# One block for the first two stages of a decoder layer, with hand-laid buffers and an early start of the second stage, and a start and an end of the experts by token tile

## What is computed

```python
x = x + attention(layernorm(x), w_qkv, w_out, alibi_slopes)        # stage 1, causal, 16 heads of 32
  probs = num / (sum(num) + 1e-6), num = 0.5 * (1 + s * rsqrt(1 + s * s))
q = layernorm(x) @ W_q;  k, v = context @ W_k, context @ W_v       # stage 2, 8 heads of 64
x = x + softmax(where(mask, q @ k.T / 8, -FLT_MAX)) @ v @ W_o + b_o
s = softmax(layernorm(x) @ w_router)                               # stage 3: top 2 of 8 experts,
x = x + sum_e weight_e * (gelu(xb_e @ w1_e) @ w2_e) + bias         # each takes 896 tokens
```

## Time and profile before

| | us |
|---|---|
| median of 3 runs | 3380.05 (3374.13 to 3383.58) |
| the profiled execution | 3391.78 |
| its span (first to last instruction) | 3390.1 |
| PE busy | 3071.0 (91%) |
| DVE busy | 1669.1 (49%) |
| ACT busy | 1351.4 (40%) |
| POOL busy | 732.2 (22%) |
| mean granted clock of PE | 0.951 of full speed |

### The profile page before, as it was taken

One profiled execution on the slowest core, in us unless ns is written; L12 is line 12 of the kernel. 1 busy time (PEld: TensorE's weight loads), 2 busy tenths in 40 slices (PEclk: granted clock), 3 DMA queues, 4 the chain that ended last, 5 costly groups with the idle time before them and its releaser, 6 DMA issues. The chain is left out here.

```text
span 3390.1 us, 52927 instructions
## 1 busy us (share of the span) xinstructions
PE 3071.0 (91%) x19340; PEld 2500.3 (74%) x19340; DVE 1669.1 (49%) x3816; ACT 1351.4 (40%) x2297; POOL 732.2 (22%) x564
## 2 busy tenths in 40 slices
PE   5889999865999999999999839999999999999997
PEld 4667777754777777777777628887888788878886
DVE  5888888843555565555555623232223232323232
ACT  5677777743555555555555411111111111111111
POOL 0000000001112222121221123333333333333333
PEclk9889999977999999999999859999999999999999
DMA  2011111114111111111110022222222222222222
GB/s 95 23 34 44 43 43 43 44 50 145 37 37 43 36 51 52 36 37 42 48 54 23 17 70 72 61 83 70 74 61 83 70 74 63 81 72 72 66 78 59
DMA packets 96191, 193.80 MB, mean 57 GB/s; under 512 B 18656, under 2 KB 28640, under 8 KB 94016
## 3 DMA queue, kind: packets, MB, share of 16 engines
q1 hardware_dynamic: 80912, 160.78, 15.6%
q0 software_dynamic: 15152, 31.26, 4.4%
HBM read 144.19 MB, written 47.82 MB: 57 GB/s over the span
## 5 line engine op out<-in xcount | busy, mean ns | idle before, releaser
L1619 DVE CAST f_hh<-f_hf 128x448 fp32r<-128x448 f32 x256 | 116.8, 456 | 893.2 <-ACT f_hf L1643 860.5
L1643 ACT ACTIVATE f_hf<-f_h 128x448 f32<-128x448 f32 x256 | 139.6, 545 | 1016.0 <-PE f_h L1679 983.2
L1566 POOL TENSOR_TENSOR f_w1l<-f_raw,f_w1h 128x512 fp32r<-128x512 f32 x130 | 183.4, 1411 | 829.2 <-DVE f_w1h L1601 829.1
L1695 PE MATMUL f_y<-f_w2h,f_hh 128*128 128x512 f32 x896 | 357.9, 399 | 0.0
L1695 PE MATMUL f_y<-f_w2h,f_hl 128*128 128x512 f32 x896 | 354.0, 395 | 0.0
L1695 PE MATMUL f_y<-f_w2l,f_hh 128*128 128x512 f32 x896 | 352.3, 393 | 0.0
L1266 ACT ACTIVATE c_s_sb<-c_s_sb,c_nmx 112x750 f32<-112x750 f32 x256 | 236.0, 922 | 188.9 <-DVE c_nmx L1095 186.5
L1679 PE MATMUL f_h<-f_xTh,f_w1h 128*128 128x448 f32 x1024 | 261.8, 378 | 32.3 <-ACT f_hf L1643 16.8
L1258 ACT COPY c_pT<-c_psum 125x672 f32<-125x672 f32 x256 | 184.7, 722 | 241.1 <-PE c_psum L1359 237.4
L1359 PEld LDWEIGHTS c_psum<-c_ident,c_s_sb 112*125 112x125 f32 x1536 | 198.2, 194 | 90.2 <-issue 84.5
L1679 PE MATMUL f_h<-f_xTl,f_w1h 128*128 128x448 f32 x1024 | 256.1, 373 | 0.0
(11 more groups left out here) (243 smaller groups left out, 5725.5 us busy)
## 6 DMA issues: line engine op xcount, KB each, us to landing
f_raw<-in_w SPq DMA_DIRECT2D x132, 512.0 KB
c_craw<-in_ctxT SPq DMA_DIRECT2D x16, 1125.0 KB, 5.1
a_x_in<-in_x SPq DMA_DIRECT2D x9, 896.0 KB, 5.7
a_xr<-in_x SPq DMA_DIRECT2D x8, 896.0 KB, 6.0
x_dram<-a_xr SPq DMA_DIRECT2D x8, 896.0 KB, 4.8
q_dram<-a_q SPq DMA_DIRECT2D x32, 224.0 KB, 5.3
c_q<-q_dram SPq DMA_DIRECT2D x16, 448.0 KB, 5.5
c_x<-x_dram SPq DMA_DIRECT2D x16, 448.0 KB, 4.6
```

What stands on the lines that cost most here:

```text
L1566: pool.tensor_tensor(w1s[1][:, n % NSLOT].rearrange("p k c -> p (k c)"), raw1[:, g % 2, n % 2, :], w1s[0][:, n % NSLOT].rearrange("p k c - ...
L1619: dve.tensor_copy(hs[0][:, l % 2, c * HC:c * HC + HC], hf[:, c, :]).then_inc(h_hi, 1)
L1643: act.activation(hf[:, c, :], H[:, 0:HC], ACT.Gelu_apprx_tanh).then_inc(free, 1)
L1695: mm = pe.matmul(Y[t][:], hs[a][:, l % 2, 128 * t:128 * t + 128], w2s[b][:, l % NSLOT, :], start=j == 0 and q == 0, stop=j == FB - 1 and q ...
```

## The change

*Buffers.* A class `Region` gives out SBUF addresses by hand, and a class `Handover` divides the memory into ten regions in which both stages lay their tensors, one over the other. It owns what is shared: the key and value weights, the context, `kT`, a separate buffer `stage` with four slots for weight pieces, the queries, the ten pieces' loads and splits, and one PSUM tensor (the units' banks are 4 and 5 for both stages, the transposes of the second stage 6 and 7). The semaphores with counts that a region is dead (`QKV_DEAD`, `outputs_dead`, `all_dead` and others) stand in place of the barrier.

*One block.* `self_attention` and `cross_attention` add their programs to one block, so each engine goes on from one to the other by itself.

*Last iteration of the first stage.* SP loads pieces 0 to 3 and the context behind `xr`. ACT rounds pieces 0 to 2 behind step 2, the context behind step 3, pieces 3 to 5 behind step 4; POOL makes the rests (DVE made both). PE does key units CK00, CK01, CK10 in step 6, CK11, CK20 in step 7 and CK21, CK30, CK31 between the last transposes. ACT takes them out. `normalise` comes before Y2 and Y3.

*Second stage.* `START` has the three value units alone, with the first scores ahead of them. Pieces 6 to 9 (output weights) are split by ACT and POOL in the first batch. The small loads and the mask are issued behind the first stage's last stores.

*Experts.* The first seven gathers have a semaphore each, and their transposes go to the seven banks `Y`. The scatters wait tile by tile for `ys_made`, each wait followed by a semaphore increment; the weight split ahead of them waits for the weight alone.

The diff, cut to its core (changes of indentation left out):

```diff
+    def load_piece(self, sp, n):
+        src, dst, k = self.pieces[n]
+        if n >= 4:
+            sp.wait_ge(self.w_lo, n - 3)
+        sp.dma_start(self.stage[:, n % 4, :], src[:, k, :]).then_inc(self.w_loaded[n % 4], 16)
+    def hi_of_piece(self, act, n):
+        src, dst, k = self.pieces[n]
+        act.wait_ge(self.w_loaded[n % 4], 16 * (n // 4 + 1))
+        act.copy(dst[0][:, k, :], self.stage[:, n % 4, :]).then_inc(self.w_hi, 1)
+    def lo_of_piece(self, pool, n):
+        pool.wait_ge(self.w_hi, n + 1)
+        pool.tensor_tensor(dst[1][:, k, :], self.stage[:, n % 4, :], dst[0][:, k, :].bitcast(F32), ALU.subtract).then_inc(self.w_lo, 1)
...
 def self_attention
-                     6: (["T2e2"], []),
-                     7: (["T2e3"], [])}
+                 6: (["T2e2"], ["CK00", "CK01", "CK10"]),
+                 7: (["T2e3"], ["CK11", "CK20"])}
-        END = ["OUT2", "OUT3", "Y0", "Y1", "Y2", "Y3", "T2c0", "T2c1", "T2c2", "T2c3", "Z0", "Z1", "Z2", "Z3"]
+    END = ["OUT2", "OUT3", "Y0", "Y1", "Y2", "Y3", "T2c0", "CK21", "T2c1", "CK30", "T2c2", "CK31", "T2c3", "Z0", "Z1", "Z2", "Z3"]
+    QKV_DEAD = (gen_full, product_number(NIT - 1, "last", "V3") + 1)
...
                     sp.dma_start(xr[:], one(x_v, i)).then_inc(xr_loaded, 16)
+            if kind == "last":
+                sp.wait_ge(x_loaded, (NIT + 1) * 16)
+                sp.wait_ge(mv_made[0], (NIT + 1) * TPI)
+                for n in range(4):
+                    handover.load_piece(sp, n)
+                sp.wait_ge(*QKV_DEAD)
+                handover.load_context(sp, 0)
...
+        for n in range(4, len(handover.pieces)):
+            handover.load_piece(sp, n)
             sp.wait_ge(stats_made[1], NIT)
             store_x1(NIT - 1)
+        sp.wait_ge(*handover.values_dead)
+        for e in range(2):
+            sp.wait_ge(q2_stored[e], 48)
+        handover.load_queries(sp, 0)
...
+                if kind == "last" and s in (2, 4):
+                    for n in range(3):
+                        handover.hi_of_piece(act, n + 3 * (s // 4))
+                if kind == "last" and s == 3:
+                    handover.hi_of_context(act, 0)
...
-            for unit in END[:6]:
+        for unit in END[:4]:
                 evacuate(NIT + 1, "end", unit)
             normalise(1, NIT - 1, xr, xn2)
...
 def cross_attention
-        START = [K(0, 0), K(0, 1), K(1, 0), K(1, 1), K(2, 0), V(0, 0), V(0, 1), V(0, 2), K(2, 1), K(3, 0)]
+    START = [V(0, 0), V(0, 1), V(0, 2)]
...
+        sp.wait_ge(*handover.outputs_dead)
             for dst, src in ((wr[:], w_r), (bo[:], b_o.partition_broadcast(R)), (bi[:], bias.partition_broadcast(R))):
                 sp.dma_start(dst, src).then_inc(small_loaded, 16)
-            sp.wait_ge(w_lo, 10)
...
             load_mask(0)
+        sp.wait_ge(*handover.all_dead)
             sp.dma_start(x1[:], x1_v[0]).then_inc(x_loaded, 16)
...
-            for unit in START:
-                evacuate(0, "start", unit)
             exponential(0, 0)
+        evacuate(0, "start", START[0])
             exponential(0, 1)
+        for unit in START[1:]:
+            evacuate(0, "start", unit)
+        for n in range(6, len(handover.pieces)):
+            handover.hi_of_piece(act, n)
...
 def experts
+                    pool.wait_ge(ys_made, it * (2 * NT) + p * NT + t + 1)
+                    pool.sem_inc(ys_seen, 1)
...
-                    if j == FB - 1:
-                        w = ((ys_made, it * (2 * NT) + NT * (p + 1)), (scattered, (it * 2 + p) * (16 * NT)))
...
-            pe.wait_ge(gathered, 16 * NT)
             for t in range(NT):
-                if t:
-                    pe.wait_ge(free, t)
-                rows(t)
+                pe.wait_ge(first_gathered[t], 16)
+                rows(t, Y[t])
```

More of the change, by code:

```diff
@@ L740, in cross_attention @@
-def cross_attention(nc, ctxT, mask, q2_dram, x1_dram, w_k, w_v, w_o, b_o, w_r, bias, out, xn_dram, table_dram):
+    sem = lambda n: ctx.enter_context(nc.semaphore("a_" + n))
+    at = lambda name: handover.region("a_", name)
+    sb = at("weights")
+    wqkv = [sb(f"wqkv{k}", [128, KC, 3 * C], F32R) for k in "hl"]
+    xT = [sb(f"xT{k}", [128, KC, TOK], F32R) for k in "hl"]
+    s_row = sb("s_row", [128, R])
+    x_in = at("rows")("x_in", [R, TPI, C])
+    ew = at("work")("ew", [128, 5 * EW])
@@ new lines, in self_attention, with units @@
+    START = ["T1c0", "T1c1", "T1c2", "T1c3", "Q0", "K0", "Q1", "K1", "V0", "V1", "Q2", "K2"]
+    END = ["OUT2", "OUT3", "Y0", "Y1", "Y2", "Y3", "T2c0", "CK21", "T2c1", "CK30", "T2c2", "CK31", "T2c3", "Z0", "Z1", "Z2", "Z3"]
+    def units(kind, s, half):
+        return [u for u in (PLAN_LAST if kind == "last" else PLAN)[s][half] if u not in NOT_YET.get(kind, ())]
+    BODIES = ("first", "second", "mid", "last")
+    ORDER = {k: [u for s in range(NG) for half in range(2) for u in units(k, s, half)] for k in BODIES}
@@ new lines, in step, with has_step, iterations @@
+    def step(i, s):
+        return (i, s) if s < NG else (i + 1, s - NG)
+    def has_step(kind, s):
+        return s < NG or kind != "last"
+    def iterations(eng, body):
+        body(0, "first")
+        body(1, "second")
+        with eng.Fori(2, NIT - 1) as i:
+            body(i, "mid")
+        body(NIT - 1, "last")
+    pieces = [(w_outT[:, k, :], wout, k) for k in range(KC)] + [(w_qT[:, k, :], wq2, k) for k in range(KC)]
+    stage = lambda n: ew[:, n * 3 * C:(n + 1) * 3 * C]
+    CONSTS = 6
@@ L741, in cross_attention @@
+def cross_attention(nc, ctx, block, handover, mask, x1_dram, b_o, w_r, bias, out, xn_dram, table_dram):
     NJ = J // JB
@@ new lines, in cross_attention, with units, has @@
+    LATE = (K(3, 1), V(1, 0), V(1, 1), V(1, 2))
+    START = [V(0, 0), V(0, 1), V(0, 2)]
+    def units(kind, s, slots=(0, 1, 2)):
+        def has(unit):
+            projection, own = unit[0] in ("K", "V"), unit[0] == "PV" and unit[1] < NM - 1
+            return {"first": (projection or own) and unit != K(3, 1), "mid": True, "last": unit in LATE or not projection, "end": not (projection or own)}[kind]
+        return [u for slot in slots for u in (PLAN[s][slot] if s in PLAN else []) if has(u)]
```

2489 lines of the change are left out of this document (1264 added, 1225 removed).

## The result

The changed kernel takes 3346.01 us (median of 4 runs, 3337.39 to 3348.83) against 3381.82 us for the kernel before (4 runs, 3374.13 to 3383.95). The ratio is 0.989, with a 95% interval of 0.9875 to 0.9905: 36 us less, where 48 were forecast. The prediction named the right sign, and its range holds the time, but its likeliest time was 14 us too low. The profiled execution took 3345.06 us, with a span of 3343.3.

A forecast was written before the change was run, and what follows sets the result against it. PE, busy 91% of the span, bounds the kernel, so time comes only from its holes or the end. Seam 29.1, experts' start 15.1 and end 3.7 sum to 47.9 us: 3343.9 profiled, 3332.2 median, range 3317 to 3347.

The forecast's parts named there:

- The loads inside the last iteration: First stage's last iteration: weight pieces queue behind the 896 KB load, so ACT goes on 8.9 us later; bounds 0 and 10.6.
- The context's splits: Step 3 of that iteration: ACT's three context splits, about 2.4 us, partly in idle time, cost 0.6 us; bounds 0 to 2.4.
- POOL beside DVE: Last iteration: POOL's splits lengthen DVE passes by up to 2.2 us each, 1.2 taken of 0 to 6.5; first batch 2.
- Key units and the seam: Between the stages: -6.6 us up to the last products, then 37.7 gained to the first transposes, mask landing in 4.0.
- The experts' start: First expert: own semaphore and PSUM bank per gathered tile let transposes follow each gather, 15.1 us gained.
- The end: Kernel's end: weight split no longer waits, first scatter 4.37 us sooner, less about 0.1 by seven: 3.7 us gained.
- The returns: Seven other expert ends: PE does not wait for POOL there, so the earlier scatters are worth nothing; loop returns forecast 0.
- The rival "slower": Both stages' loops: one block brings return stalls, 17 x 4.2 = 71 us lost, 3403.6 us; chance 0.03.
- The starting point: Whole kernel: profiled execution lies 11.7 us above the median of three runs, so 3343.9 becomes a median of 3332.2.

## Why the prediction was right, and where it was wrong

*The loads inside the last iteration.* Forecast 8.9 us of stall; the step took 19.20 us instead of 10.23, so 9.0. The run that issues the pieces some 18 us sooner removes the stall, which shows that ACT waited for these loads; by itself it doesn't show a queue, since it makes them earlier as well. For the queue speaks how long pieces of one size take to land, in the view of tile h_stage from 660 to 700 us of the changed kernel:

```profile
DMA to landing us min/median/max: 3.2/6.8/7.3
```

The four behind the 896 KB load took 6.8 to 7.3 us, the three issued from 694 us on, when the large loads had landed, 3.2 to 3.8. The context's splits were forecast to cost 0.6 us; the trace gives them nothing of their own.

*POOL beside DVE.* Forecast 1.2, with bounds 0 and 6.5. The next two steps took 11.17 and 10.48 us, 1.28 and 0.55 more than before, and each excess is that of one pass of L504 (1.65 and 0.95 against 0.39). 1.8 us, then, 0.6 more than forecast, and as the context cost 0.6 less, the two errors cancel: the iteration is 10.8 us longer in all (10.7 forecast). That sum was luck in part. The upper bound that it spoke for was far off, since most passes run without POOL beside them, and the price of 2.2 us a pass was a maximum: in the trace of before 50 of the 256 passes of L1081 overlap one of POOL's, and three took over 1 us. In the first batch the stretch to the second mask pass cost 2.6 us (forecast 2), and up to 4.3 in other profiles; how much of it is POOL's doing no run separates.

*Key units and the seam.* -5.4 and 39.0 against -6.6 and 37.7, closer than these rows repeat. The mask landed 5.1 us behind its issue, not 4.0, and the issues began 3.0 us behind the last product's end (3.2 forecast). In return the third value unit and the next scores took 6.0 us (783.37 to 789.37) and not 7.1, so here too errors cancel. PE's hole of 5.66 us ends, as written, when ACT has freed a bank behind the first exponential.

*The experts' start.* 14.7 against 15.1: right in size, though the banks and the semaphores had not been told apart.

*The end.* This term failed: 3.7 us forecast, 0.2 measured. The scatters do start 4.4 us sooner, the last like the first, so that their seven waits and increments cost nothing; but I ended the count at POOL's last scatter and not at what closes the block. The DRAIN behind it was in the trace of before (14.0 us, ending 0.7 us behind the last landing). With the new start it ends 4.3 us later behind the landing; that, no row of before shows.

*The returns.* This is the other failed step, the sentence that the end is worth nothing at the other ends, since PE doesn't wait for POOL there: 0 forecast, 9.7 us lost. PE doesn't wait for POOL; but at three of these ends it waits for its own code, and the scatters and weight loads now reach the DMA engines first. The earlier trace rows had the place and its price, and I used it for a rival about other loops instead of asking what the earlier transfers would collide with. The rival "slower" named the return as the mechanism; the seam's loops show no such stall, the experts' loop shows it 3.2 us dearer three times. The two failed terms make 13.2 us of the forecast's excess; the others together came out 1.5 us better than forecast.

*The starting point.* The profiled execution was 11.7 us above its median, and I subtracted that from the sum. That was sound: the terms hold between events, not against an execution's own total.

## What to carry to other kernels

A transfer that is made earlier lands among other transfers: look for what is fetched in the same microseconds, and count the code of an engine that returns to the top of a long loop among it. Compare two profiles by stretches between events: here those repeat to tenths of a us, at the seam to 1 or 2, while fourteen unchanged batches alone moved by up to 29. And follow a saving at the end to the last instruction of the block, not to the last one of the kernel's own.

## What the runs showed of the hardware

- A return to the top of the experts' loop stops PE for 3.8 to 4.4 us with the DMA engines idle up to the instruction packet (15 returns), 5.0 to 5.3 us with 1 MB of weight loads under way (3), 6.5 to 7.5 us with scatters besides (24). The one packet of the instruction queue comes 1.2 to 1.8 us into the hole in the first case, 2.4 to 2.6 in the second and 3.9 to 4.8 in the last, and the first product 2.6 to 3.1 us behind it in all.
- POOL's DRAIN at the end of the block ends 0.7 us behind the last landing of its scatters when all gathers signal one semaphore (5 profiles), and 5.0 us behind it when the first seven signal one each (9).
- Fourteen batches of one stage, the same code, took 992 to 1021 us in fourteen profiles.
